# A graph layer on one core: the last codes matched ahead of the next one-hots, and the next block's rows turned ahead of the unit's sums

## The reference

```python
h = jnp.maximum(_layernorm(x, axis=-1), 0.0)
msgs = h[src]
agg = jax.ops.segment_sum(msgs, dst, num_segments=n)
deg = jax.ops.segment_sum(jnp.ones((src.shape[0],)), dst, num_segments=n)
agg = agg / jnp.maximum(deg, 1.0)[:, None]
t = jax.nn.relu(agg @ Wg + h @ Ws + bg)
t = jnp.tanh(t @ W1 + b1)
t = jnp.tanh(t @ W2 + b2)
return x + (t @ W3 + b3)
```

## Time and profile before

| | us |
|---|---|
| median of three runs (2009.32 to 2025.4) | 2015.59 |
| the profiled execution | 2000.25 |
| its span in the trace | 1998.4 |
| TensorE matmuls busy | 1377.6 (69%) |
| VectorE busy | 1040.4 (52%) |
| GpSimd busy | 901.1 (45%) |
| ScalarE busy | 574.1 (29%) |

### The profile page before, as it was taken

One profiled execution on the slowest core, in us unless ns is written; L12 is line 12 of the kernel. 1 busy time (PEld: TensorE's weight loads), 2 busy tenths in 40 slices (PEclk: granted clock), 3 DMA queues, 4 the chain that ended last, 5 costly groups with the idle time before them and its releaser, 6 DMA issues.

```text
span 1998.4 us, 26207 instructions
## 1 busy us (share of the span) xinstructions
PE 1377.6 (69%) x8920; PEld 1053.1 (53%) x8920; DVE 1040.4 (52%) x2581; ACT 574.1 (29%) x1195; POOL 901.1 (45%) x948
## 2 busy tenths in 40 slices
PE   1206488659674988648866989568764989547888
PEld 1104356437553766436644767446643777436667
DVE  8715455428452776426642776427632767426531
ACT  7203043204220442203221433214220433213232
POOL 0473346363645355462546354553635245552530
PEclk8558779779887999778977999879977999878989
DMA  7211212112212122111212122121211122112210
GB/s 266 101 57 53 68 40 85 36 56 62 86 40 77 31 80 87 39 48 60 88 38 80 39 81 81 44 61 55 86 33 56 58 80 85 44 45 64 85 37 9
DMA packets 79023, 130.78 MB, mean 65 GB/s; under 512 B 20462, under 2 KB 58944, under 8 KB 74800
## 3 DMA queue, kind: packets, MB, share of 16 engines
q0 software_dynamic: 29952, 61.40, 10.7%
q1 hardware_dynamic: 48670, 66.09, 10.2%
q10 hardware_dynamic: 274, 1.60, 0.3%
HBM read 115.96 MB, written 13.05 MB: 65 GB/s over the span
## 4 chain that ended last, share of the span: by engine, by line
PE 58%; another core or an unknown queue 24%; issue 9%; ACT 6%; DVE 2%; DMA 1%; DVEq 0%; SPq 0%; ACTq 0%
PE banks L789 15%; PE banks L736 11%; PE banks L751 11%; PE banks L655 6%; PE banks L803 5%; PE banks L772 4%; PE banks L761 2%; PE banks L764 2%; ACT arena L1096 1%; PE banks L707 1%; ACT arena L1011 1%; ACT dense L1075 1%; DMA xin<-in_x_dram 1%; ACT dense L1068 0%
## 5 line engine op out<-in xcount | busy, mean ns | idle before, releaser
L593 POOL DMA_INDIRECT ring<-h_table,idx_all x936 | 899.3, 961 | 1030.7 <-PE banks L789 276.4
L789 PE MATMUL banks<-dense,w 128*128 128x256 f32 (+1 forms) x1568 | 452.3, 407 | 125.7 <-ACT dense L1075 71.8
L736 PE MATMUL banks<-xin,arena 128*128 128x256 f16 (+1 forms) x1960 | 297.1, 287 | 132.3 <-ACT arena L1096 69.7
L789 PEld LDWEIGHTS banks<-dense,w 128*128 128x128 f32 x1568 | 279.9, 204 | 174.6 <-ACT dense L1075 74.1
L1096 ACT CAST arena<-banks 128x512 f16<-128x512 f32 (+1 forms) x500 | 274.2, 581 | 229.7 <-PE banks L736 125.9
L736 PEld LDWEIGHTS banks<-xin,arena 128*128 128x128 f16 (+1 forms) x1960 | 188.1, 102 | 210.1 <-ACT arena L1096 82.2
L751 PE MATMUL banks<-arena 128*128 128x257 f16 x1960 | 257.2, 291 | 31.3 <-issue 30.8
L1479 DVE TENSOR_SCALAR arena<-node,qd 128x256 f16<-128x256 f16 x980 | 201.4, 290 | 95.0 <-PE banks L751 91.8
L751 PEld LDWEIGHTS banks<-arena 128*128 128x128 f16 x1960 | 200.9, 104 | 81.9 <-issue 41.6
L655 PE MATMUL banks<-ring,onehot 128*128 (+1 forms) x1102 | 219.4, 288 | 4.6 <-issue 4.3
L1075 ACT ACTIVATE dense<-banks,b2c 128x256 f32<-128x256 f32 (+1 forms) x196 | 92.8, 476 | 414.2 <-remote 249.7
(11 more groups left out here) (126 smaller groups left out, 971.3 us busy)
## 6 DMA issues: line engine op xcount, KB each, us to landing
arena<-unit_codes SPq DMA_DIRECT2D x20, 1568.0 KB
ring<-h_table,idx_all POOLq DMA_INDIRECT x936
xin<-in_x_dram SPq DMA_DIRECT2D x6, 1024.0 KB, 18.1
h_table<-xin SPq DMA_DIRECT2D x6, 1024.0 KB, 4.2
tblk<-h_table SPq DMA_DIRECT2D x48, 128.0 KB
xblk<-in_x_dram SPq DMA_DIRECT2D x48, 128.0 KB
out_dram<-dense SPq DMA_DIRECT2D x48, 128.0 KB
w<-in_L_gnn_W_dram SPq DMA_DIRECT2D x1, 1024.0 KB, 7.3
```

Of the source, the lines that this page charges most:

```text
L593: nc.gpsimd.indirect_dma_start(out=ring_tiles[:, t % RING, 0:2 * D], out_offset=None, in_=table, in_offset=bass.IndirectOffsetOnAxis(ap=id ...
L736: mm = nc.tensor.matmul(to, wide_l[0:rows, piece % WSLOTS, k, j, :], tab[0:rows, 2 * g + j, :], start=(j == 0), stop=(j == 1))
L789: mm = nc.tensor.matmul(l3_ps[c][:, 0:w], w2[:, q, c * P:(c + 1) * P], h2T[:, q, 0:w], start=(q == 0), stop=(q == HC - 1))
```

## The change

In a period of `tensor`, `turn(PLACE[following])` and its six matmuls stand ahead of all of the unit's sums rather than between pieces 5 and 6, in periods 1 to 18. In a period of `vector`, `match_codes(n, [7])` stands between `finish` and `make_onehot` of the first segment rather than behind both, in periods 1 to 19. No instruction is added or removed.

```diff
@@ tensor, period(n)
                 turn_out(kt)
                 turn_codes(n + 1)
-                sum_unit(n, range(NP - 2), hand_over=(4,) if spread else ())
                 following = PERIODS[n + 1][1][0]
                 turn(PLACE[following])
-                sum_unit(n, [NP - 2])
+                sum_unit(n, range(NP - 1), hand_over=(4,) if spread else ())
                 layer1(following, PLACE[following])
                 sum_unit(n, [NP - 1], hand_over=(NP - 1,) if spread else ())
@@ vector, period(n)
                 match_codes(n, [6])
-                step(steps[0])
+                finish(steps[0])
                 match_codes(n, [7])
+                make_onehot(steps[0] + 2)
```

## The result

The changed kernel has a median of 2032.51 us (2021.43 to 2058.31, 20 runs), the kernel before 2015.49 (2002.21 to 2026.2, 20 runs): a ratio of 1.0088, 95% interval 1.0064 to 1.0113, so 17 us slower. The forecast was 2029.6.

What follows compares the result with a forecast made beforehand. PE bounds 58% of the chain, 24% is waits read as signals held behind POOL's gathers; 20.5 us lost less 6.5 gained is 14, added to the 2015.6 median: 2029.6 us, 8-in-10 range 2001 to 2042.

Steps and rivals of the forecast that it cites:

- The reading of the 24%: Chain share under an unnamed releaser: PE's signals late in a run of gathers reach others 1 to 2 us after its end.
- Part A: The turn moved ahead of the unit's sums on PE: 6.5 us gained, bounds 0 and 13.6.
- the tie: End of short periods: layer 1's activation is tied to POOL's run of gathers, whose start follows from piece 4.
- The 0.45 of PE: The turn's PE time, 0.45 us in each of 18 periods, moves into the wait for the turned codes.
- rival 3: Part A joins runs too: piece 7's first matmul raises `quarter_free` inside a run, four more gathers follow; 2050 us, chance 0.08.
- The 2 us for the long periods: Part A's gain in seven long periods: 0.0 to 0.2 in five, 0.45 in two, together 2.
- Part B: Piece 7 ahead of the one-hots on DVE: pair 21's 1.24 us wait goes, but runs join; 20.5 us lost, bounds 7 to 27.
- F: Short periods 3, 6, 10, 13, 16: POOL pauses after four gathers; mean 41.5 us from pair 0 to the codes' turn.
- G: Short periods 5, 8, 11, 15, 18: eight gathers without a pause; mean 46.2 us from pair 0 to the codes' turn.
- The price of a joined run: G's length less F's, 4.7 us, less 0.6 for the earlier run start: 4.1 us in each of five periods.
- That costs nothing: On DVE the one-hots end 1.26 us later, but everything behind them starts when it did.
- Rival 1: The runs of gathers don't join: Part B keeps its 6.2 us gain and Part A its 6.5; 2003 us, chance 0.25.

Runs made afterwards that it cites:

- part A alone: Kernel before with only the turn moved ahead of all the unit's sums: 1.0046 on chip 8; 0.9961 on chip 5, 0.9966 on chip 4.

## Why the prediction was right, and where it wasn't

**The time** was right, 2029.6 against 2032.5, and so was the sign, on chips that hold signals. That was luck: 20.5 lost and 6.5 gained were recorded, and the parts alone cost 9 each. One term was 11 too high, the other 15.5 too low, and the errors nearly cancelled.

**The reading of the 24%** held. Signals of PE leave 1 to 2 us behind a run of gathers, and the loss came from there. The prediction did not see that this belongs to some chips and not to others. That it is the gathers that hold them is still inferred: no run took the gathers away.

**Part A, recorded as 6.5 us gained, costs 9** (chip 8). The step that failed is "whose start follows from piece 4 of the sums, which stays where it is". Piece 4 does not stay. The turn's six matrix instructions now stand ahead of it, in the stretch where PE gets through only a few at a time while the gathers run, and the hand-over in piece 4 releases the next four gathers. Layer 1's activation is tied to the end of those. The prediction had the tie right and then did not follow it back to its start. The 0.45 of PE was counted as free because it lies in a wait, and in that wait it does cost nothing; it costs behind it. What it named as the gain, the wait ahead of layer 1, did go. In the change as a whole, these ends cost 12.9 in the profiled executions: 0.83 later for layer 2 in eleven periods, and 3.8 behind layer 2 in period 11 alone, where rival 3 came true. That the turn's place costs is shown by three kernels. That it works through the hand-over in piece 4 is read from the timelines (the gathers start 1.1 behind it in both kernels) and not tried by itself, and the kernel with the turn behind piece 2 agrees with it only in part. The 2 us for the long periods are also the top of their own terms, which give 0.9 to 1.9.

**Part B, recorded as 20.5 us lost, costs 9** (chip 7, inside the bounds of 7 to 27). The step "so I expect F to turn into G" came true there in all five periods, but on the first chip in period 16 alone. In period 10 of after, a new wait of 0.75 for ACT's copy ahead of slot 14 ate part of the 1.24: slot 14 started 3.76 behind the run's start (1134.61 against 1130.85) and 0.9 before its end, where 3.5 and 1.2 were forecast. That does not explain the rest.

In periods 3, 6 and 13 of after slot 14 was at 3.42, as forecast, and the gathers paused for 1.4 to 1.8; in period 16, and in period 3 on chip 7 (479.11 against 475.68), it was at 3.42 and they joined; on chip 8 they joined at 3.7. So the step that failed is "In G it is raised 3.4 after the start (934.98 against 931.56), and is seen in time", taken as a rule for F: the place of slot 14 in the run does not settle whether the hand-over is seen. What does is open.

The price of a joined run was mis-sized too, 4.1 recorded against 2.3 on chip 7. It was taken from the periods of one execution in which kind G was dear (mean 46.2; 43.6 on chip 7), and it goes with the granted clock: G takes 43.55 at 1.00, 44.68 at 0.96 and 47.19 to 48.21 at 0.93. The one run that joined in F on the first chip cost 6.5, at 0.93.

**"That costs nothing" on DVE** held: with nothing held, part B is a plain gain of 12 us. **Rival 1** is what happens on those chips, with 0.9892 for its 0.994; the rule of the Trainium skill that the trace of before spoke against agrees with the traces of chips 4 and 5. **Rival 3**, at a chance of 0.08, did occur: in period 11 of after, and with part A alone on chip 8 in periods 6 and 8, where the next quarter followed after 0.8 and pair 0 waited 1.0. In most of the other short periods with the turn ahead of piece 4 the hand-over of piece 7 fell into the run as well, 3.8 to 4.5 behind its start, and was not seen before its end.

**The marks.** L736's wait for the codes was gone, as said. Eight gathers and 43 to 47 us in kind F: only period 16 has the run, and it took 48.2. In the four others POOL still paused between the quarters of slots 10 and 14, which was the recorded sign of being wrong. No idle time ahead of layer 1 behind the sums: right. Layer 2 no sooner: right, and later.

## What to carry to other kernels

Work that is put into a wait is free only if nothing late in the same instruction row releases another engine; follow the first signal behind the new place, not only the one that it was moved away from. Before pricing a small change of order from one trace, look whether its waits have a releaser that the profile can name. If not, the verdict may hold for one chip: here the same pair of edits was 0.9% slower on one and 1.1% faster on another. And a forecast that comes out right may still be two wrong terms: run each part alone.

## What the runs showed of the hardware

The kernel before takes 2015 us where the result was taken, 2009, 1974 and 1973 on chips 13, 8 and 7 (the first may be one of these), and 1384 on chips 4 and 5. The mean granted clock of the profiled executions is 0.84 to 0.86 on the slower ones and 0.96 on the two others. On the slower ones PE's signals are late while POOL gathers: of 1571 signals of one execution 547 to 593 come over 0.3 us after the matmul's end in the trace (579 in that of before), on the two others 10 to 25. On the slower ones PE also stops in such a run without a releaser in the profile, some 36 to 40 matmuls behind the turn of the codes, and goes on in groups about 0.7 us apart. The gathers take the same time on both kinds (961 and 974 ns). What makes a chip one or the other no run here shows.
